# Dynamic filter's taps multiplied for two chunks at once, with the first two pairs' sums copied by the scalar engine and added by GpSimd

## The chip, the cores and the metric

The kernel runs on one core of one Trainium2 chip. The metric is the device time of one execution in microseconds (us). The engines are called PE (matmul), DVE (vector), ACT (scalar), POOL (GpSimd) and SP (sync, which issues the transfers here).

## The reference

The input x is (8, 64, 56, 56). Four layers follow each other, each as x = x + layer(groupnorm(x)):

- layer 0, the dynamic filter: nine taps t of a 3x3 window; the output is the sum over t of patch_t(x) * cf[b, c, t] * sf[b, t, pixel]. cf is a filter per channel from a small network on the pooled x, sf a filter per pixel from a 1x1 convolution. Both are normalised over the nine taps.
- layer 1: a 1x1 convolution times a sigmoid attention map.
- layer 2: a 3x3 convolution with ternary weights.
- layer 3: softmax attention over all 3136 pixels.

```python
def _ddf_mul(x, cf, sf):
    xp = jnp.pad(x, ((0, 0), (0, 0), (1, 1), (1, 1)))
    out = jnp.zeros((B, C, H, W), x.dtype)
    for u in range(3):
        for v in range(3):
            patch = xp[:, :, u:u + H, v:v + W]
            out = out + patch * cf[:, :, u, v][:, :, None, None] * sf[:, u * 3 + v][:, None]
    return out
```

## The kernel before

Two images of 64 channels fill the 128 partitions, so the batch of 8 is four groups, g = 0 to 3 (a loop for the first three, the last written out). Each group runs layers 0 to 3 in turn. An image of 3136 pixels is cut into NJ = 7 chunks of CH = 448 pixels (8 rows of 56); a chunk fills most of one PSUM bank of 512 float32. Engines are kept in step by semaphores written out by hand; each engine works through its own list in order.

The stage that is changed is the tap stage of layer 0. For each chunk j:

- PE spreads the pixel filter of tap t over the channels (`spread_tap`, L1161: one bf16 matmul into bank t % 3). A spread waits for the product three taps earlier, which frees its bank.
- DVE multiplies it by cf and by the shifted patch of the padded input (`tap`, L595: one SCALAR_TENSOR_TENSOR of 448 elements from PSUM and xnp, into the slice `prod[t]`, which lies in the tile Pb).
- PE adds the products of the even taps (0, 2, 4, 6, 8) in PSUM by matmuls with the identity (`add_tap`, L1169: float32, two passes each). Two banks take turns by chunk (`ACCB + odd`).
- POOL adds the odd taps (1, 3, 5, 7) and the layer's input xin in four additions (L1024, L1026, L1029, L1033; `pu`, which lies in the tile VT).
- DVE adds the two sums into xw (`l0_sum`, L605), between taps 3 and 4 of the next chunk.

There is one `prod` slice for each tap. The product of a tap may be written again for the next chunk when its reader has added the one before: PE for even taps, POOL's first addition for taps 1 and 3, the third for tap 5, the fourth for tap 7. After the last chunk DVE takes the group norm statistics of xw (L484, one per chunk; then L489), and the short chain of layer 1's norm follows: PE (L1106, L1110), DVE, POOL (L1013), DVE (L503). ACT has no work in the tap stage except to load its table for layer 1 (L842). `keep_busy` (L1148) issues matmuls whose result nobody reads while that chain runs. Layer 1 then normalises on ACT (L834) and multiplies on PE (L1204, L1205).

Of the kernel before, what the change touches and what calls it, by code (L numbers as in the profile page):

```python
# [166 lines left out]
def build(nc, x, weights, vectors, cst, out):  # L167
    with ExitStack() as ctx:
# [17 lines left out]
        selb = sb("selb", [3 * PITCH, TAPS, P], BF16)  # L186
# [18 lines left out]
        cf = sb("cf", [P, TAPS])  # L205
# [99 lines left out]
        tap_ready = sem("tap_ready")  # L305
# [4 lines left out]
        l0_done = sem("l0_chunk_done")  # L310
        km_ps = sem("km_in_psum")
        km_ready = sem("km_ready")
        u_ps = sem("u_in_psum")
# [128 lines left out]
        def _(dve):  # L442
# [40 lines left out]
            def chunk_stats(src, j):  # L483
                return nc.vector.bn_stats(st6[:, j, :], src[:, j * CH:(j + 1) * CH])  # L484
# [96 lines left out]
            def group(g, more):  # L581
                n[0] = FRONT_LINKS


                def tap(j, t):
                    k = NJ * g + j
                    dve.wait_ge(tap_ready, TAPS * k + t + 1)

                    if t % 2 == 0:
                        dve.wait_ge(tap_added, PE_TAPS * k + t // 2 + 1)  # L590
                    elif t < 7:
                        dve.wait_ge(pool_step, POOL_STEPS * k + (1 if t < 5 else 3))
                    else:
                        dve.wait_ge(pooltaps, k + 1)
                    nc.vector.scalar_tensor_tensor(  # L595
                        out=rows(prod[:, t, :]), in0=rows(PS[:, t % TAP_BANKS, 0:CH]), scalar=cf[:, t:t + 1],
                        in1=pad_rows_at(xnp, j * (ROWS * PW) + (t // 3) * PW + t % 3, ROWS),
                        op0=ALU.mult, op1=ALU.mult).then_inc(prod_ready, 1)

                def l0_sum(j, odd):  # L600

                    dve.wait_ge(tap_added, PE_TAPS * (NJ * g + j + 2))
                    dve.wait_ge(pooltaps, NJ * g + j + 2)
                    dve.wait_ge(stored, 16 * (NJ * g + 1))
                    nc.vector.tensor_tensor(xw[:, ds(j * CH, CH)], PS[:, ACCB + odd, 0:CH], pu[:, 2, :],  # L605
                                            ALU.add).then_inc(l0_done, 1)

                for t in range(TAPS):
                    tap(0, t)
                with dve.Fori(0, NJ // 2) as i:  # L610
                    for odd in (1, 0):
                        j = 2 * i + 2 - odd
                        for t in range(TAPS):
                            if t == 4:
                                l0_sum(j - 1, 1 - odd)
                            tap(j, t)
                dve.wait_ge(l0_done, NJ * (g + 1) + 1)
                for i in range(NJ - 2):
                    chunk_stats(xw, i)
                l0_sum(NJ - 1, 0)  # L620
                chunk_stats(xw, NJ - 2)


                dve.wait_ge(l0_done, NJ * g + NJ + 2)
                stats(g, 1, chunk_stats(xw, NJ - 1))
# [202 lines left out]
        def _(act):  # L828
# [170 lines left out]
        def _(pool):  # L999
# [95 lines left out]
        def _(pe):  # L1095
            mm = nc.tensor.matmul
            pe.sem_inc(tap_added, PE_TAPS)
            pe.sem_inc(l0_done, 2)
            pe.wait_ge(w_loaded, 3 * 16)
            pe.wait_ge(consts, 2)  # L1100
            pe.wait_ge(setup, 1)
# [42 lines left out]
            def group(g, more):  # L1144
# [9 lines left out]
                    pair_var(g, layer, small)  # L1154
                    keep_busy(meanwhile)

                def spread_tap(j, t):

                    k = NJ * g + j
                    pe.wait_ge(prod_ready, TAPS * k + t + 1)  # L1160
                    mm(PS[:, t % TAP_BANKS, 0:CH], selb[:, t, :], SF[:, ds(j * CH, CH)],  # L1161
                       start=True, stop=True).then_inc(tap_ready, 1)

                def add_tap(j, odd, t):
                    k = NJ * g + j
                    pe.wait_ge(prod_ready, TAPS * k + t + 1 + TAP_BANKS)
                    if t == 0:
                        pe.wait_ge(l0_done, k + 1)
                    mm(PS[:, ACCB + odd, 0:CH], identf, prod[:, t, :], start=(t == 0),  # L1169
                       stop=(t == TAPS - 1)).then_inc(tap_added, 1)  # L1170

                def taps(j, odd, first):
                    for t in range(TAPS):
                        spread_tap(j, t)
                        if t in (1, 2) and not first:
                            add_tap(j - 1, 1 - odd, 4 + 2 * t)
                        if t in (3, 5, 7):
                            add_tap(j, odd, t - 3)

                pe.wait_ge(SF_ready, NJ * (g + 1))  # L1180
                taps(0, 0, True)
                with pe.Fori(0, NJ // 2) as i:
                    taps(2 * i + 1, 1, False)
                    taps(2 * i + 2, 0, False)
# [270 lines left out]
```

## Time and profile before

| | us |
|---|---|
| median of three runs (1804.43 to 1806.83) | 1804.92 |
| the profiled execution, its own time | 1803.89 |
| its span, first to last instruction | 1802.0 |
| busy in the span: PE, DVE, ACT, POOL | 1643.3, 1240.5, 1212.8, 1101.6 |
| tap stage with the norm behind it, from the first tap to the end of L503, groups 0 to 3 | 50.16, 52.14, 51.74, 49.06 |

The span is cut into engine busy times; a busy PE is not PE at its peak, since matmuls are pipelined and overlap. Most of the span is layer 3's attention. The four tap stages take 203 us together, 11% of it. PE has two clock levels, 2.4 and 1.2 GHz: the column PEclk of a stretch is its granted share, 1.00 or 0.50 for a stretch at one level.

### The profile page before, as it was taken

The page shows a single profiled execution, that of the slowest core. Times are in us where ns is not written, and L with a number is a line of the kernel's source. Part 1 is how long each engine was busy: PE and PEld are TensorE (multiplying, and loading weights), DVE is VectorE, ACT ScalarE, POOL GpSimd, SP SyncE. Part 2 cuts the span into 40 slices and gives each one's busy share as a digit, 9 for nine tenths or more (in the row PEclk, how much of TensorE's full clock was granted, in tenths as well). Part 3 has the DMA queues.
Part 4 walks back from the last instruction along what each step waited for, and adds up shares of the span by engine and source line. Part 5 has one row for each costly group of instructions (what it writes and reads, how often), then busy time and mean ns, then how long its engine had stood idle before and what let it go on. Part 6 is the DMA issues. An engine that isn't in the chain of part 4 may idle for free.

```text
span 1802.0 us, 35669 instructions
## 1 busy us (share of the span) xinstructions
PE 1643.3 (91%) x10892; PEld 835.9 (46%) x10892; DVE 1240.5 (69%) x2443; ACT 1212.8 (67%) x2300; POOL 1101.6 (61%) x926
## 2 busy tenths in 40 slices
PE   5987899999889799999988879999998788999997
PEld 4364444444436345444444634444443364444442
DVE  5946777775584777777367478777738648877760
ACT  2045889998403689999731278999972237899995
POOL 2720488789551058888955106888887402688888
PEclk9989999999989899999988899999999899999999
DMA  2004000000000400000000040000000002000000
GB/s 87 0 1 90 2 7 7 7 7 11 8 0 1 90 2 7 7 7 7 12 8 0 1 90 2 7 7 11 8 7 6 0 20 35 2 12 6 7 7 11
DMA packets 12423, 27.16 MB, mean 15 GB/s; under 512 B 4560, under 2 KB 8912, under 8 KB 11728
## 3 DMA queue, kind: packets, MB, share of 16 engines
q1 hardware_dynamic: 12240, 24.92, 5.9%
q8 instruction: 90, 1.47, 0.4%
q14 instruction: 93, 0.76, 0.1%
HBM read 8.73 MB, written 6.42 MB: 8 GB/s over the span
## 4 chain that ended last, share of the span: by engine, by line
PE 59%; issue 15%; POOL 10%; DVE 9%; ACT 6%; POOLq 1%; DVEq 0%; ACTq 0%
PE PS L1315 26%; PE PS L1271 12%; PE PS L1241 12%; DVE nmt L688 4%; ACT Pb L956 2%; POOL VT L1024 2%; POOL VT L1029 2%; POOL VT L1026 2%; PE PS L1213 2%; DVE nmt L681 2%; POOL VT L1033 2%; ACT PS L911 1%; PE PS L1204 1%; POOL accP L1076 1%; PE PS L1205 1%
## 5 line engine op out<-in xcount | busy, mean ns | idle before, releaser
L681 DVE TENSOR_REDUCE nmt<-PS 128x1 f32<-128x448 f32 x1176 | 681.6, 618 | 211.0 <-PE PS L1241 208.0
L1076 POOL TENSOR_TENSOR accP<-accP,Pb 128x512 f32<-128x512 f32 (+1 forms) x532 | 676.7, 1272 | 125.9 <-ACT Pb L956 97.5
L956 ACT ACTIVATE Pb<-PS 128x896 f32<-128x896 f32 (+1 forms) x700 | 637.5, 915 | 128.5 <-PE PS L1271 118.9
L1315 PE MATMUL PS<-Pb,VT 128*64 128x448 f32 x2800 | 659.9, 544 | 4.8 <-ACT Pb L956 4.1
L1241 PE MATMUL PS<-Ka,Qa 96*64 96x448 bf16 x2888 | 499.8, 358 | 23.6 <-ACT PS L911 10.7
L1271 PE MATMUL PS<-Qa,Ka 99*64 99x448 bf16 x2744 | 491.7, 353 | 3.3 <-ACT Pb L956 2.8
L911 ACT ACTIVATE PS<-PS,nmt 128x448 f32<-128x448 f32 x588 | 356.6, 606 | 30.6 <-DVE nmt L688 28.6
L1241 PEld LDWEIGHTS PS<-Ka,Qa 96*64 96x64 bf16 x2888 | 168.3, 110 | 270.9 <-issue 117.6
L1271 PEld LDWEIGHTS PS<-Qa,Ka 99*64 99x64 bf16 x2744 | 168.4, 110 | 241.8 <-issue 187.4
L1315 PEld LDWEIGHTS PS<-Pb,VT 128*64 128x64 f32 x2800 | 194.9, 137 | 102.6 <-ACT Pb L956 30.3
L834 ACT ACTIVATE xnp<-xw,nb,rstd 128x448 f32<-128x448 f32 x56 | 40.5, 750 | 204.5 <-DVE nb L503 204.5
L1069 POOL TENSOR_TENSOR accQ<-Pb 128x512 f32<-128x512 f32 x28 | 35.6, 1270 | 226.4 <-ACT Pb L956 226.4
L595 DVE SCALAR_TENSOR_TENSOR Pb<-PS,cf,xnp 128x448 f32<-128x448 f32 x252 | 154.8, 676 | 17.1 <-PE PS L1161 11.8
L1169 PE MATMUL PS<-Pb,cs 128*128 128x448 f32 x280 | 134.0, 560 | 0.7 <-DVE Pb L595 0.7
L1076 POOL TENSOR_TENSOR accQ<-accQ,Pb 128x512 f32<-128x512 f32 x84 | 106.6, 1269 | 23.0 <-ACT Pb L956 19.0
L911 ACT ACTIVATION_READ_ACCUMULATOR PS<-PS,nmt 128x1 f32 x588 | 117.0, 199 | 0.0
L1013 POOL TENSOR_TENSOR rstd<-ve,mhalf 128x1 f32<-128x1 f32 x16 | 8.8, 548 | 169.5 <-DVE ve L499 169.3
L688 DVE TENSOR_REDUCE nmt<-PS 128x1 f32<-128x448 f32 x196 | 104.7, 607 | 1.5 <-PE PS L1241 1.5
L1161 PE MATMUL PS<-xnf,selb 96*128 (+1 forms) x252 | 83.7, 369 | 15.4 <-issue 6.6
L834 ACT ACTIVATE xnf<-xw,nb,rstd 128x448 f32<-128x448 f32 x28 | 20.7, 752 | 102.5 <-DVE nb L503 102.5
L730 DVE STREAM_TRANSPOSE Rr<-PS 128x448 f32<-128x448 f32 x28 | 18.2, 650 | 72.3 <-PE PS L1285 72.3
L1161 PEld LDWEIGHTS PS<-xnf,selb 96*128 96x128 bf16 x252 | 24.6, 98 | 92.2 <-DVE Pb L595 52.9
(145 smaller groups left out, 1478.4 us busy)
## 6 DMA issues: line engine op xcount, KB each, us to landing
xin<-in_x SPq DMA_DIRECT2D x4, 1568.0 KB, 11.9
out<-xw SPq DMA_DIRECT2D x28, 224.0 KB, 1.9
Qa<-parts SPq DMA_DIRECT2D x24, 168.0 KB, 7.6
Ka<-parts SPq DMA_DIRECT2D x24, 112.0 KB, 3.8
Ka<-parts SPq DMA_DIRECT2D x24, 84.0 KB, 2.6
Qa<-mpt SPq DMA_DIRECT2D x96, 1.3 KB
wz<-in_weights SPq DMA_DIRECT2D x1, 829.0 KB, 8.2
Qa<-parts SPq DMA_DIRECT2D x24, 28.0 KB, 1.9
```

Source lines behind the costliest of these rows:

```text
L595: nc.vector.scalar_tensor_tensor(out=rows(prod[:, t, :]), in0=rows(PS[:, t % TAP_BANKS, 0:CH]), scalar=cf[:, t:t + 1], in1=pad_rows_at(xnp ...
L681: nc.vector.reduce_max(nmt[:, target % 2, b, t:t + 1], PS[0:BLK, bank, 0:CH], X, negate=True).then_inc(mx_free, 1)
L688: nc.vector.reduce_max(nmt[:, 0, b, t:t + 1], PS[0:BLK, i % NJ, 0:CH], X, negate=True).then_inc(first_used, 1)
L834: nc.scalar.activation(dst, rows(src[:, j * CH:(j + 1) * CH]), ACT.Identity, bias=nb[:, :], scale=rstd[:, :]).then_inc(done, 1)
L911: return nc.scalar.activation(PS[0:BLK, bank, 0:CH], PS[0:BLK, bank, 0:CH], ACT.Exp, bias=nmt[:, target % 2, b, t:t + 1], accum_out=sm[:, ...
L956: nc.scalar.activation(Pb[0:r, j % PSLOTS, :, :], PS[0:r, 2 * (k % 2):2 * (k % 2) + 2, 0:CH], ACT.Exp).then_inc(exp_done, 1)
L1076: nc.gpsimd.tensor_tensor((accQ if j < TO_ACCP else accP)[0:r, :, REST:CH], (accQ if j <= TO_ACCP else accP)[0:r, :, REST:CH], Pb[0:r, j % ...
L1161: mm(PS[:, t % TAP_BANKS, 0:CH], selb[:, t, :], SF[:, ds(j * CH, CH)], start=True, stop=True).then_inc(tap_ready, 1)
L1169: mm(PS[:, ACCB + odd, 0:CH], identf, prod[:, t, :], start=(t == 0), stop=(t == TAPS - 1)).then_inc(tap_added, 1)
L1241: last = mm(PS[C * h:C * h + C, bank, 0:CH], Qa[0:KROWS, h, s * CH + b * C:s * CH + b * C + C], Ka[0:KROWS, h, t * CH:(t + 1) * CH], start ...
L1271: ins = mm(PS[c:c + C, 2 * (k % 2) + h, 0:CH], Ka[0:KROWS + 3, h, j * QC + c:j * QC + c + C], Qa[0:KROWS + 3, h, s * CH:(s + 1) * CH], sta ...
L1315: last = mm(PS[C * h:C * h + C, OB, 0:CH], VT[:, j, C * h:C * h + C], Pb[:, j % PSLOTS, h, :], start=(j == 0), stop=(j == NQ - 1))
```

## The change

- The seven chunks become four units: `UNITS = ((0, 1), (2, 3), (4, 5), (6,))`. A tap of DVE is one instruction over both chunks of a unit (896 elements over two PSUM banks), the last unit's over one.
- The spread of a unit is two matmuls into a pair of banks; three pairs (banks 0 to 5) take turns as the three banks did.
- The even taps of a unit are added in one pair of banks, 6 and 7, for all units. Before, two single banks took turns.
- That pair must be emptied before the next unit's first even tap is added. For units 0 and 1 (`COPIED = 2`) ACT copies it to SBUF (`acc`, 896 elements) and POOL adds it to its own sum and writes xw; for units 2 and 3 DVE's `l0_sum` does both as before.
- POOL's four additions are of 896 elements for units 0 to 2. Those of the first two units' sums stand behind its second addition of the next unit.
- The products are nine slices of 896 elements: five in Pb, and accP, accD and two pieces of Qa, which are free in this stage.
- DVE takes the statistics of units 0 and 1 between taps 6 and 7 of units 2 and 3, those of units 2 and 3 after the last tap.
- PE adds even taps in another order: 0 and 2 of a unit behind spreads 4 and 6, 4 behind spread 8, and 6 and 8 behind the next unit's spreads 0 and 1.
- The inner loops over chunks are gone from DVE, POOL and PE; the units are written out.

```diff
-TAP_BANKS = 3
+TAP_SLOTS = 3
+UNITS = ((0, 1), (2, 3), (4, 5), (6,))
+COPIED = 2
...
-        prod = flat[:, 0:TAPS * CH].rearrange("p (t n) -> p t n", t=TAPS)
+        prod = [Pb[:, t, :, :] for t in range(PSLOTS)]
...
-        pu = flat[:, 0:3 * CH].rearrange("p (a n) -> p a n", a=3)
+        pu = flat[:, 0:6 * CH].rearrange("p (a h n) -> p a h n", a=3, h=2)
...
-        att, gated = accP, accD
+        att, gated, acc = accP, accD, accQ
+        prod += [accP, accD] + [Qa[:, h, 0:4 * CH].bitcast(F32).rearrange("p (h n) -> p h n", h=2) for h in range(2)]
...
-        ACCB = 4
+        ACCB = 6
...
+                for u in range(len(UNITS)):
+                    for t in range(TAPS):
+                        if t == 5 and u > COPIED:
+                            l0_sum(u - 1)
+                        if t == 7 and u >= 2:
+                            l0_stats(u - 2)
+                        tap(u, t)
+                l0_stats(len(UNITS) - 2)
+                l0_sum(len(UNITS) - 1)
+                stats(g, 1, l0_stats(len(UNITS) - 1))
...
             def group(g, more):
+                for u in range(COPIED):
+                    act.wait_ge(tap_added, PE_TAPS * (len(UNITS) * g + u + 2))
+                    if u:
+                        act.wait_ge(l0_done, len(UNITS) * g + u)
+                    nc.scalar.activation(acc[:, :, :], PS[:, ACCB:ACCB + 2, 0:CH], ACT.Copy).then_inc(acc_copied, 1)
                 load_table(ACT.Sigmoid)
...
+                    nc.gpsimd.tensor_tensor(part[0], prod[1][:, 0:m, :], prod[3][:, 0:m, :], ALU.add).then_inc(pool_step, 1)
...
+                    nc.gpsimd.tensor_tensor(part[1], part[0], x, ALU.add).then_inc(pool_step, 1)
+                    if 1 <= u <= COPIED:
+                        l0_sum(u - 1)
...
+                    nc.gpsimd.tensor_tensor(part[0], part[1], prod[5][:, 0:m, :], ALU.add).then_inc(pool_step, 1)
...
+                    if u:
+                        pool.wait_ge(l0_done, len(UNITS) * g + u)
+                    nc.gpsimd.tensor_tensor(part[2], part[0], prod[7][:, 0:m, :], ALU.add).then_inc(pooltaps, 1)
...
+                def add_tap(u, t):
+                    k = len(UNITS) * g + u
+                    pe.wait_ge(prod_ready, TAPS * k + t + 1 + TAP_SLOTS)
+                    if t == 0 and u == 0:
+                        pe.wait_ge(ocopy, NJ * g + 1)
+                        pe.wait_ge(recip, NJ * g + 1)
+                    elif t == 0 and u <= COPIED:
+                        pe.wait_ge(acc_copied, COPIED * g + u)
+                    elif t == 0:
+                        pe.wait_ge(l0_done, len(UNITS) * g + u)
+                    for i in range(len(UNITS[u])):
+                        last = mm(PS[:, ACCB + i, 0:CH], identf, prod[t][:, i, :], start=(t == 0), stop=(t == TAPS - 1))
+                    last.then_inc(tap_added, 1)
...
+                        spread_tap(u, t)
+                        if u and t in (0, 1):
+                            add_tap(u - 1, 6 + 2 * t)
+                        if t in (4, 6):
+                            add_tap(u, t - 4)
+                        elif t == TAPS - 1:
+                            add_tap(u, 4)
```

## Rows read from the trace of the kernel before

**Rows 1.** The page: engine, busy us, share of the span, instructions.

```profile
PE 1643.3 (91%) x10892; PEld 835.9 (46%) x10892; DVE 1240.5 (69%) x2443; ACT 1212.8 (67%) x2300; POOL 1101.6 (61%) x926
```

**Rows 2.** Busy time by stretch: the tap stages of groups 0 and 3.

```profile
core 0: us, PE busy (x) PEld busy (x) DVE busy (x) ACT busy (x) POOL busy (x), PEclk, DMA share, GB/s
42.62:92.78 50.16, 44.90 (x139) 19.43 (x137) 46.76 (x84) 0.66 (x2) 32.29 (x29) 0.98 0.00 0
...
1368.10:1417.16 49.06, 43.08 (x137) 18.56 (x137) 46.60 (x85) 0.14 (x1) 34.52 (x31) 0.98 0.01 5
```

**Rows 3.** The same view: one chunk in the middle of the stage.

```profile
60.00:66.04 6.04, 5.90 (x20) 2.60 (x19) 6.03 (x11) 0.00 (x0) 4.54 (x5) 1.00 0.00 0
```

**Rows 4.** The chain that ended last, same stretch: start, us, what.

```profile
63.27 0.81 issue
64.12 1.14 POOL VT L1024
```

**Rows 5.** Timeline of DVE: start, us, what, number; its first tap and one chunk.

```profile
42.62 2.65 DVE L595 SCALAR_TENSOR_TENSOR Pb<-PS,cf,xnp 128x448 f32<-128x448 f32 x4 [3.31 <-PE PS L1161]
...
52.41 5.59 DVE L595 SCALAR_TENSOR_TENSOR Pb<-PS,cf,xnp 128x448 f32<-128x448 f32 x9
57.92 0.61 DVE L605 TENSOR_TENSOR xw<-PS,VT 128x448 f32 x1
```

**Rows 6.** Timeline of PE at half and at full clock.

```profile
43.70 1.70 PE L1169 MATMUL PS<-Pb,cs 128*128 128x448 f32 x2
...
57.01 0.92 PE L1169 MATMUL PS<-Pb,cs 128*128 128x448 f32 x2
57.76 0.54 PE L1161 MATMUL PS<-xnf,selb 96*128 x2
```

**Rows 7.** Groups by line and shape, DVE, whole span: count, busy us, mean ns.

```profile
L595 DVE SCALAR_TENSOR_TENSOR Pb<-PS,cf,xnp 128x448 f32<-128x448 f32 x252 | 154.8, 676 | 17.1 <-PE PS L1161 11.8 <-issue 3.6
...
L653 DVE TENSOR_TENSOR xl<-xnp,xh 128x448 fp32r<-128x448 f32 x28 | 17.6, 628 | 22.2 <-ACT xnp L834 22.1
...
L473 DVE TENSOR_TENSOR wt<-wz,Pb 128x1152 fp32r<-128x1152 f32 x1 | 1.4, 1360 | 0.0
```

**Rows 8.** The same view for POOL.

```profile
L1076 POOL TENSOR_TENSOR accP<-accP,Pb 128x512 f32<-128x512 f32 x504 | 641.4, 1273 | 120.0 <-ACT Pb L956 92.8
...
L1033 POOL TENSOR_TENSOR VT<-VT,Pb 128x448 f32<-128x448 f32 x28 | 31.8, 1135 | 6.6 <-POOL VT L1029 6.6
...
L1056 POOL TENSOR_TENSOR sme<-sm,ef 128x21 f32<-128x21 f32 x28 | 6.5, 232 | 0.0
```

**Rows 9.** Timeline of POOL in the tap stage.

```profile
45.35 1.13 POOL L1024 TENSOR_TENSOR VT<-Pb 128x448 f32<-128x448 f32 x1 [6.69 <-DVE Pb L595]
...
53.36 1.13 POOL L1026 TENSOR_TENSOR VT<-VT,xin 128x448 f32<-128x448 f32 x1 [0.19 <-POOL VT L1024]
54.65 1.13 POOL L1029 TENSOR_TENSOR VT<-VT,Pb 128x448 f32<-128x448 f32 x1 [0.16 <-POOL VT L1026]
56.01 1.14 POOL L1033 TENSOR_TENSOR VT<-VT,Pb 128x448 f32<-128x448 f32 x1 [0.23 <-POOL VT L1029]
```

**Rows 10.** The page's groups: ACT on 896 elements of two PSUM banks.

```profile
L956 ACT ACTIVATE Pb<-PS 128x896 f32<-128x896 f32 (+1 forms) x700 | 637.5, 915 | 128.5 <-PE PS L1271 118.9
```

**Rows 11.** Timeline of DVE behind the last tap.

```profile
85.55 2.72 DVE L484 BATCH_NORM_STATS2 st<-xw 128x6 f32<-128x448 f32 x5
88.19 0.61 DVE L605 TENSOR_TENSOR xw<-PS,VT 128x448 f32<-128x448 f32 x1
88.71 1.14 DVE L484 BATCH_NORM_STATS2 st<-xw 128x6 f32<-128x448 f32 x2
```

**Rows 12.** Timeline of PE: three of its idle gaps (in brackets) in group 0.

```profile
90.29 0.38 PE L1106 MATMUL PS<-mv,cs 128*128 128x1 f32 x2 [3.58 <-DVE mv L489]
...
111.04 0.38 PE L1106 MATMUL PS<-mv,cs 128*128 128x1 f32 x2 [3.69 <-DVE mv L489]
...
145.55 0.50 PE L1106 MATMUL PS<-mv,cs 128*128 128x1 f32 x2 [2.22 <-DVE mv L489]
```

**Rows 13.** Busy time by stretch: behind those three gaps.

```profile
91.10:97.80 6.70, 6.26 (x17) 3.24 (x18) 1.15 (x8) 2.71 (x4) 0.55 (x1) 0.50 0.00 1
...
111.60:118.30 6.70, 6.03 (x18) 3.98 (x18) 2.43 (x7) 4.74 (x8) 0.55 (x1) 0.50 0.00 0
...
145.70:152.40 6.70, 6.39 (x15) 2.18 (x16) 1.31 (x5) 2.60 (x4) 0.55 (x1) 0.50 0.00 0
```

More of the change, by code:

```diff
@@ L309, in build @@
         pooltaps = sem("pool_taps_summed")
-        l0_done = sem("l0_chunk_done")
+        acc_copied = sem("tap_sums_copied")
+        l0_done = sem("l0_unit_done")
         km_ps = sem("km_in_psum")
@@ L582, in group, with tap @@
                 n[0] = FRONT_LINKS
-                def tap(j, t):
-                    k = NJ * g + j
+                def tap(u, t):
+                    k, m = len(UNITS) * g + u, len(UNITS[u])
                     dve.wait_ge(tap_ready, TAPS * k + t + 1)
@@ L594, in tap @@
                         dve.wait_ge(pooltaps, k + 1)
+                    b = 2 * ((TAPS * u + t) % TAP_SLOTS)
+                    x = pad_rows(xnp, UNITS[u][0] * ROWS + t // 3, m * ROWS, t % 3)
                     nc.vector.scalar_tensor_tensor(
-                        out=rows(prod[:, t, :]), in0=rows(PS[:, t % TAP_BANKS, 0:CH]), scalar=cf[:, t:t + 1],
-                        in1=pad_rows_at(xnp, j * (ROWS * PW) + (t // 3) * PW + t % 3, ROWS),
+                        out=prod[t][:, 0:m, :].rearrange("p h (r w) -> p h r w", w=W),
+                        in0=PS[:, b:b + m, 0:CH].rearrange("p h (r w) -> p h r w", w=W), scalar=cf[:, t:t + 1],
+                        in1=x.rearrange("p (h r) w -> p h r w", h=m),
@@ L598, in tap, with l0_sum @@
                         op0=ALU.mult, op1=ALU.mult).then_inc(prod_ready, 1)
-                def l0_sum(j, odd):
-                    dve.wait_ge(tap_added, PE_TAPS * (NJ * g + j + 2))
-                    dve.wait_ge(pooltaps, NJ * g + j + 2)
+                def l0_sum(u):
+                    j, m = UNITS[u][0], len(UNITS[u])
+                    dve.wait_ge(tap_added, PE_TAPS * (len(UNITS) * g + u + 2))
+                    dve.wait_ge(pooltaps, len(UNITS) * g + u + 2)
                     dve.wait_ge(stored, 16 * (NJ * g + 1))
-                    nc.vector.tensor_tensor(xw[:, ds(j * CH, CH)], PS[:, ACCB + odd, 0:CH], pu[:, 2, :],
-                                            ALU.add).then_inc(l0_done, 1)
@@ L608, in group @@
[L608 to L625, printed above, removed]
+                    nc.vector.tensor_tensor(xw[:, j * CH:(j + m) * CH].rearrange("p (h n) -> p h n", h=m),
+                                            PS[:, ACCB:ACCB + m, 0:CH], pu[:, 2, 0:m, :], ALU.add).then_inc(l0_done, 1)
+                def l0_stats(u):
+                    dve.wait_ge(l0_done, len(UNITS) * g + u + 1)
+                    for j in UNITS[u]:
+                        last = chunk_stats(xw, j)
+                    return last
@@ L1019, in group, with l0_sum @@
             def group(g, more):
-                with pool.Fori(0, NJ) as j:
-                    k = NJ * g + j
+                def l0_sum(u):
+                    j = UNITS[u][0]
+                    pool.wait_ge(acc_copied, COPIED * g + u + 1)
+                    pool.wait_ge(pooltaps, len(UNITS) * g + u + 2)
+                    pool.wait_ge(stored, 16 * (NJ * g + 1))
+                    nc.gpsimd.tensor_tensor(xw[:, j * CH:(j + 2) * CH].rearrange("p (h n) -> p h n", h=2),
+                                            acc[:, :, :], pu[:, 2, :, :], ALU.add).then_inc(l0_done, 1)
@@ L1022, in group @@
+                for u in range(len(UNITS)):
+                    k, j, m = len(UNITS) * g + u, UNITS[u][0], len(UNITS[u])
+                    x = xin[:, j * CH:(j + m) * CH].rearrange("p (h n) -> p h n", h=m)
+                    part = [pu[:, a, 0:m, :] for a in range(3)]
                     pool.wait_ge(pooltaps, k + 1)
-                    pool.wait_ge(prod_ready, TAPS * k + 4 + TAP_BANKS)
-                    nc.gpsimd.tensor_tensor(pu[:, 0, :], prod[:, 1, :], prod[:, 3, :], ALU.add).then_inc(pool_step, 1)
+                    pool.wait_ge(prod_ready, TAPS * k + 4 + TAP_SLOTS)
+                    nc.gpsimd.tensor_tensor(part[0], prod[1][:, 0:m, :], prod[3][:, 0:m, :], ALU.add).then_inc(pool_step, 1)
@@ L1029, in group @@
-                    nc.gpsimd.tensor_tensor(pu[:, 0, :], pu[:, 1, :], prod[:, 5, :], ALU.add).then_inc(pool_step, 1)
+                    pool.wait_ge(prod_ready, TAPS * k + 6 + TAP_SLOTS)
+                    nc.gpsimd.tensor_tensor(part[0], part[1], prod[5][:, 0:m, :], ALU.add).then_inc(pool_step, 1)
                     pool.wait_ge(pool_step, POOL_STEPS * (k + 1) + 3)
-                    pool.wait_ge(prod_ready, TAPS * k + 8 + TAP_BANKS)
-                    pool.wait_ge(l0_done, k + 2)
-                    nc.gpsimd.tensor_tensor(pu[:, 2, :], pu[:, 0, :], prod[:, 7, :], ALU.add).then_inc(pooltaps, 1)
+                    pool.wait_ge(prod_ready, TAPS * k + 8 + TAP_SLOTS)
@@ L1155, in pair_stats, with spread_tap @@
                     keep_busy(meanwhile)
-                def spread_tap(j, t):
-                    k = NJ * g + j
+                def spread_tap(u, t):
+                    k = len(UNITS) * g + u
                     pe.wait_ge(prod_ready, TAPS * k + t + 1)
[L1161 to L1170, printed above, removed]
@@ L1172, in taps @@
-                def taps(j, odd, first):
-                    for t in range(TAPS):
[L1174 to L1184, printed above, removed]
@@ L1185, in group @@
-                add_tap(NJ - 1, 0, TAPS - 3)
-                add_tap(NJ - 1, 0, TAPS - 1)
+                    for i, j in enumerate(UNITS[u]):
+                        last = mm(PS[:, 2 * ((TAPS * u + t) % TAP_SLOTS) + i, 0:CH], selb[:, t, :],
+                                  SF[:, j * CH:(j + 1) * CH], start=True, stop=True)
+                    last.then_inc(tap_ready, 1)
+                def add_tap(u, t):
+                    k = len(UNITS) * g + u
+                    pe.wait_ge(prod_ready, TAPS * k + t + 1 + TAP_SLOTS)
[9 more added lines that the diff above has]
+                    last.then_inc(tap_added, 1)
@@ new lines, in group @@
+                pe.wait_ge(SF_ready, NJ * (g + 1))
+                for u in range(len(UNITS)):
+                    for t in range(TAPS):
+                        spread_tap(u, t)
[5 more added lines that the diff above has]
+                            add_tap(u, 4)
+                add_tap(len(UNITS) - 1, 6)
@@ L1189, in group @@
+                add_tap(len(UNITS) - 1, 8)
                 pair_stats(1, 2)
```

5 lines of the change are left out of this document (1 added, 4 removed).

## The prediction

> **What bounds the kernel now.** I began with the page [rows 1]: PE is busy 91% of the span, but the change touches only the tap stages, so their limit has to be read there. The busy times by stretch give four stages of 49 to 52 us [rows 2] (the first and last of the four); DVE is busy 46.6 to 46.8 us of each, PE 43 to 45, POOL 32 to 35. In one chunk of 6.04 us in the middle [rows 3] DVE is busy 6.03, PE 5.90, POOL 4.54. The chain of waits runs through POOL's additions there [rows 4], but POOL has spare time (1.5 us a chunk) and DVE none, so I take DVE as the limit, PE as almost level with it, and POOL as third. The timeline of DVE [rows 5] gives the interval at which it starts taps: the nine taps take 5.59 us, which holds one stall of 0.18 for PE; (5.59 - 0.18 - 0.68) / 8 = 0.59 us. The sum L605 holds it another 0.53. Everything below is a price list for three engines that stand close together: what counts is which one comes out last.
>
> **DVE.** Its trace has no tap of 896 elements. A TENSOR_TENSOR takes 628 ns for 448 elements and 1360 for 1152 [rows 7]: 1.04 ns for one more element. So a tap of a pair ends 0.676 + 0.467 = 1.14 us after its start and the next can start 0.59 + 0.47 = 1.06 after. Bounds: 1.06 (that slope) to 1.18 (two taps of before, no gain). I take 1.06, since it is one stream of the same kind. Saved: 0.12 us for each of 27 taps, 3.4 us a stage. Of the seven sums (0.53 each, 3.7) DVE keeps one of a pair and one single (0.99 + 0.53): 2.2 saved. The statistics are moved, not removed.
>
> The Trainium skill ("VectorE: DVE Perf Modes", section on the TRN2 errata) charges a fixed term for each vector instruction beside one cycle an element, and advises tiles of 512 elements or more. By its PSUM figure a pair's tap is 1.06 us as well; this trace agrees for 448 (0.59). Read alone, it speaks for the change, by the whole 5.6 us a stage.
>
> **PE.** Two passes of an addition start 0.38 apart and spreads 0.19 apart at full clock [rows 6] (the ends of two less 0.54 and 0.35). A pair of chunks needs 18 spreads and 20 passes before and after: 18 x 0.19 + 20 x 0.38 = 11.0 us, against the 12.1 that two chunks take now. So 1.1 us a pair is all that can be won while PE is in step, not DVE's 2.5.
>
> **POOL.** Additions take 1.135 us for 448 elements and 1.273 for 512, and 0.232 for 21 [rows 8]: 2.16 ns an element by the near pair, 2.11 by the far one. 896 elements cost 2.08 to 2.10 us; at most 2.27 (two of before). With the gap of 0.16 to 0.23 to the next dependent addition [rows 9], 2.28 each. Units 1 and 2 now have five such additions each, since the sums of units 0 and 1 came to POOL: 11.4 us. That is more than PE's 11.0 and more than DVE's 9.5 to 10.6. POOL becomes the pace of units 1 and 2.
>
> The same skill's "GPSIMD Engine Reference", section Elementwise, gives a GpSimd add of 2048 elements as 4497 ns against 2293 on the vector engine and says to keep elementwise work on the latter. An estimate from that page is 2.06 us for 896: the trace agrees within 2%, and ten additions would end 0.4 us earlier, which changes nothing below.
>
> **ACT.** A copy of 896 elements costs about 0.92 us [rows 10] (another function over the same kind of bank pair). It starts when a unit's tap 8 is added, behind spread 1 of the next, and ends near spread 4, before PE needs the banks: hidden by the spreads and DVE's multiplications. The table load behind both copies has over 20 us of idle ACT to hide in.
>
> **One stage, step by step** (0 = first tap, group 0's clock).
> 1. Unit 0: tap 3 ends at 3 x 1.06 + 1.14 = 4.3; POOL's four additions run from 4.4 to 13.3. DVE's nine taps end at 10.0, with 0.4 lost to PE.
> 2. Unit 1: tap 0 starts at 10.1. Taps 1 and 2 start only at 12.0 and 13.9: in PE's order the four passes of products 6 and 8 (1.5 us each) stand before spreads 1 and 2. Tap 3 ends at 16.05.
> 3. POOL starts its unit 1 at 16.1 and is not idle again before unit 3: ten additions (four of unit 1, four of unit 2, the sums 0 and 1) at 2.28, the last without its gap, end at 38.7. Products 5 and 7 are there in time.
> 4. DVE has multiplied taps 0 to 4 of unit 3 by 37.4 and then waits for POOL in `l0_sum(2)`: 38.9 to 40.0. Queued behind it on DVE are taps 5 to 8; waiting for it on PE is the first addition of unit 3, since the accumulator pair is the only one. PE's last spread ended at 35.7, so PE is idle for 4.3 us.
> 5. Then PE adds product 0 (0.76), spreads tap 5 (0.35), DVE multiplies taps 5 and 6, takes two statistics (1.1), multiplies 7 and 8, PE adds 8, DVE sums (0.61) and takes the last statistic: 7.2 us, end at 47.2.
>
> Before, from the first tap (42.62) to the end of the last statistic (88.71 + 1.14) it is 47.2 us [rows 5, 11]. What the pairs win (11.4 for 12.1) and the shorter tail wins (2.4 us behind the last tap instead of 4.2) goes in the late start of POOL's unit 1 and the stop in unit 3. The first tap itself starts 0.2 to 0.4 us later, as two spreads stand ahead of it (at half clock in group 0, [rows 6]). The same steps with the clocks of the other groups give 0.4, 0.8 and 0.7. Sum: +0.4 +0.4 +0.8 +0.7 = **+2.2 us**, if PE keeps its clock.
>
> **The clock.** After idle gaps of 3.58, 3.69 and 2.22 us [rows 12] the granted clock was 0.50, the 1.2 GHz level, for 6.7 us or more [rows 13]; the half-clock stretches begin 2.4 to 4.4 us behind the start of their gaps. The gap of step 4 (4.3 us) is longer than all three, so I expect the fall at about 38 to 40, and the half clock to last until 45 to 47. All of step 5 then runs on a slow PE: an addition takes 1.5 instead of 0.76 [rows 6]. Of the 7.2 us PE's own work is 10 passes and 4 spreads, 4.6 us, 9.1 at half clock. Followed through, the end moves to 48.7 (fall at 38.0) to 49.5 (at 40): +1.5 to 2.3, I take +1.9 a stage, **+7.6 us** in all. The layer 1 stage starts in half clock now [rows 13]; behind the new tail the gap is 1.9 us instead of 3.6, so it may escape that, worth 4 passes x 0.38 = 1.5 us a stage; or the second fall comes later and covers more of it. I take nothing.
>
> The Trainium skill's "TensorE: Matmul & The Clock Gate", section on HAM oscillation, says that a PE waiting in every tile re-throttles and starts each next one cold; the gap rows agree here (0.50 after all three). By it the price is paid in all four groups, which is my sum; without it the sum stays at +2.2.
>
> **Sum.** +2.2 + 7.6 = +9.8 against the profiled execution's own 1803.9 (span 1802.0): 1813.7. The median of the runs lies 1.0 above that execution, so 1814.7. With the small chance of relief in layer 1 I say 1814.
>
> **The rivals.** A change under 0.2%, 3.6 us, can't be told from none.
> - *Forecast*: POOL paces units 1 and 2, PE waits in unit 3, its clock falls. +5 to +15 us: 1810 to 1820. Chance 0.58.
> - *The gap but no fall, or the fall paid back in layer 1*: for it, the gap sits between stretches of full work, while those of [rows 12] are followed by small matmuls; against it, its length. +2.2, down to -1: about 1806. Chance 0.22.
> - *PE sets the pace, faster*: it decides if an addition of 896 elements costs POOL 1.85 us or less, against 2.08 from both slopes. Then `l0_sum(2)` ends with DVE's own queue, at 38.4 instead of 40.0, which is -1.6 against step 4; the four stages come to -4.2, and 1800.7, if the clock holds too (PE's gap is still 2.7 us). Chance 0.08.
> - *The change does what the instruction counts say*: DVE stays the limit, 5.6 x 4 = -22 us, 1782. It needs PE under 9.6 us a pair, against 11.0. Chance 0.04.
> - *Worse*: the written-out code or the shared accumulator adds stops that I don't see, or half clock reaches through layer 1 as well (+1.5 to 3 a stage more): 1820 to 1826. Chance 0.08.
>
> Faster by over 0.2%: 0.12; within: 0.22; slower: 0.66. The range runs from 1804 (below the second case, without the faster ones) to 1820; the likeliest case alone has 1810 to 1820.
>
> **What would show it.** After the change: taps of 1.14 us, POOL additions near 2.10 us, ten in a row with gaps of 0.2 and not idle from tap 3 of unit 1 on; a DVE wait for POOL before L605's first instance; an idle PE of about 4 us in front of the first addition of unit 3, ended by DVE; PEclk 0.50 in the stretch behind it; a stage about 2 us longer in each group. Wrong would be: a POOL idle in unit 2 (then PE or DVE leads), a gap under 2 us, or a clock of 1.00 behind it.

## The result, and the profile after

The changed kernel took 1809.49 us (median of 10 runs, 1808.10 to 1811.42) beside 1805.94 us of the kernel before (10 runs). The ratio is 1.0022, 95% interval 1.0012 to 1.0031: slower by 0.2%, 3.5 to 4 us. A repeat on another chip gave 1809.4 beside 1804.28, ratio 1.0026 (1.0015 to 1.0036). The forecast was 1814, 9 us slower. The direction was right; the size was not: 3.5 us, and 5.1 in the repeat, for 9. The time lies inside the stated range, just under its likeliest part, 1810 to 1820.

The page has the sums. DVE's busy time fell by 22 us against [rows 1], and nothing was won by it:

```profile
PE 1650.7 (91%) x10892; PEld 844.9 (47%) x10892; DVE 1218.1 (67%) x2315; ACT 1222.9 (68%) x2311; POOL 1108.6 (61%) x886
```

The four tap stages by stretch, from the first tap to the end of the norm chain, the lines that answer to [rows 2]. They end 0.07 us later in the chain than those (at L633, behind L507):

```profile
core 0: us, PE busy (x) PEld busy (x) DVE busy (x) ACT busy (x) POOL busy (x), PEclk, DMA share, GB/s
42.99:94.58 51.59, 45.18 (x138) 20.96 (x136) 41.52 (x52) 3.44 (x6) 34.07 (x19) 0.93 0.00 1
486.43:539.21 52.78, 45.41 (x138) 20.53 (x136) 41.53 (x52) 3.35 (x5) 34.09 (x19) 0.89 0.02 5
933.27:986.03 52.76, 45.58 (x138) 21.04 (x136) 41.53 (x52) 3.35 (x5) 34.07 (x19) 0.88 0.02 5
1374.51:1423.57 49.06, 41.41 (x134) 19.32 (x134) 41.11 (x53) 3.35 (x5) 36.37 (x21) 0.96 0.01 5
```

DVE is busy 5.1 to 5.5 us less in each (41.5 for 46.7), close to the 5.6 by instruction counts, and yet three stages are 0.6 to 1.4 us longer and the fourth is level. A tap of a pair takes 1.14 us, and the next starts 1.05 to 1.06 behind it, both as forecast:

```profile
60.55 1.14 DVE L601 SCALAR_TENSOR_TENSOR accP<-PS,cf,xnp 128x896 f32<-128x896 f32 x1
61.60 1.14 DVE L601 SCALAR_TENSOR_TENSOR accD<-PS,cf,xnp 128x896 f32<-128x896 f32 x1
```

POOL's timeline, group 0, units 1 and 2 and the start of unit 3, answers to [rows 9]:

```profile
59.65 2.09 POOL L1047 TENSOR_TENSOR VT<-Pb 128x896 f32<-128x896 f32 x1 [3.43 <-DVE Pb L601]
61.81 2.08 POOL L1049 TENSOR_TENSOR VT<-VT,xin 128x896 f32<-128x896 f32 x1
63.86 2.08 POOL L1038 TENSOR_TENSOR xw<-accQ,VT 128x896 f32<-128x896 f32 x1
65.91 2.08 POOL L1054 TENSOR_TENSOR VT<-VT,accP 128x896 f32<-128x896 f32 x1
68.20 2.09 POOL L1059 TENSOR_TENSOR VT<-VT,Qa 128x896 f32<-128x896 f32 x1 [0.22 <-POOL VT L1054]
70.73 2.09 POOL L1047 TENSOR_TENSOR VT<-Pb 128x896 f32<-128x896 f32 x1 [0.43 <-DVE Pb L601]
...
79.28 2.07 POOL L1059 TENSOR_TENSOR VT<-VT,Qa 128x896 f32<-128x896 f32 x1 [0.22 <-POOL VT L1054]
81.52 1.13 POOL L1047 TENSOR_TENSOR VT<-Pb 128x448 f32<-128x448 f32 x1 [0.17 <-POOL VT L1059]
```

An addition of 896 elements takes 2.08 us, as forecast. The five of unit 1 start 59.65 and those of unit 2 start 70.73: 11.08 us. POOL waited 0.43 us for a tap at that place, so POOL is not the pace alone; the run e4_noxin below shows that PE is level with it. The last addition of unit 2 ends 38.4 us behind the first tap (forecast 38.7). What waits for it is seen on DVE and then on PE:

```profile
79.14 1.87 DVE L601 SCALAR_TENSOR_TENSOR Pb<-PS,cf,xnp 128x448 f32<-128x448 f32 x3 [0.96 <-PE PS L1187]
81.58 1.09 DVE L613 TENSOR_TENSOR xw<-PS,VT 128x896 f32<-128x896 f32 x1 [0.58 <-POOL VT L1059]
85.15 0.68 DVE L601 SCALAR_TENSOR_TENSOR accP<-PS,cf,xnp 128x448 f32<-128x448 f32 x1 [2.48 <-PE PS L1187]
```

```profile
78.65 0.73 PE L1187 MATMUL PS<-xnf,selb 96*128 96x448 bf16 x3
82.82 1.83 PE L1202 MATMUL PS<-Pb,cs 128*128 128x448 f32 x2 [3.43 <-DVE xw L613]
84.44 0.95 PE L1187 MATMUL PS<-xnf,selb 96*128 96x448 bf16 x2
```

PE stands idle for 3.43 us, released by DVE's sum. Its two passes then take 1.83 us, the 1.70 of half clock [rows 6] rather than the 0.92 of full; DVE in turn waits 2.48 us for tap 5's spread. The stretches behind the gap in groups 0 and 1, each followed by the next:

```profile
81.90:88.60 6.70, 5.78 (x10) 2.79 (x11) 4.22 (x8) 0.00 (x0) 3.46 (x4) 0.50 0.00 1
88.70:95.40 6.70, 3.78 (x17) 1.58 (x15) 3.67 (x13) 0.85 (x2) 1.13 (x2) 1.00 0.00 1
95.60:102.20 6.60, 6.60 (x13) 3.12 (x13) 1.13 (x3) 2.95 (x5) 0.67 (x1) 0.50 0.00 0
...
529.10:532.30 3.20, 3.20 (x7) 1.21 (x6) 1.79 (x4) 0.00 (x0) 1.55 (x2) 0.50 0.00 0
532.50:539.10 6.60, 3.97 (x15) 1.63 (x13) 4.82 (x14) 0.00 (x0) 1.68 (x2) 1.00 0.00 1
539.30:546.00 6.70, 6.70 (x15) 3.42 (x16) 1.14 (x5) 3.66 (x6) 0.00 (x0) 0.50 0.00 0
```

The clock falls as forecast, but in group 1 it is back after 3.4 us, and so it was in groups 2 and 3. The last row of each three is layer 1, where it falls again, later than in the kernel before: compare 95.60 to 102.20 with 91.10 to 97.80 [rows 13]. The fall comes over 4 us later, though the norm chain ends only 1.7 us later.

### The profile page after: what moved, and what is told of

Its sections match the earlier page's. It is cut to its first block, busy times and chain, and to the rows that moved or that the text cites. A ratio compares the mean times of both kernels' runs of the same rounds, so it can differ in the third digit from the quotient of the medians.

```text
span 1809.6 us, 34535 instructions
## 1 busy us (share of the span) xinstructions
PE 1650.7 (91%) x10892; PEld 844.9 (47%) x10892; DVE 1218.1 (67%) x2315; ACT 1222.9 (68%) x2311; POOL 1108.6 (61%) x886
## 4 chain that ended last, share of the span: by engine, by line
PE 66%; issue 13%; DVE 9%; ACT 6%; POOL 5%; DVEq 0%; ACTq 0%; POOLq 0%
PE PS L1345 26%; PE PS L1301 12%; PE PS L1271 12%; PE PS L1202 4%; DVE nmt L695 4%; PE PS L1187 2%; ACT Pb L968 2%; PE PS L1243 2%; DVE nmt L688 2%; PE PS L1234 2%; POOL accP L1102 1%; ACT PS L923 1%; PE PS L1235 1%; PE PS L1153 1%; PE PS L1256 1%
## 5 line engine op out<-in xcount | busy, mean ns | idle before, releaser
L1345 PEld LDWEIGHTS PS<-Pb,VT 128*64 128x64 f32 x2800 | 195.8, 137 | 102.4 <-ACT Pb L968 30.2
L601 DVE SCALAR_TENSOR_TENSOR Pb<-PS,cf,xnp 128x896 f32<-128x896 f32 (+1 forms) x80 | 78.8, 1028 | 26.0 <-PE PS L1187 25.8
L1202 PE MATMUL PS<-Pb,cs 128*128 128x448 f32 x168 | 82.0, 608 | 13.5 <-DVE xw L613 13.5
L1187 PE MATMUL PS<-xnf,selb 96*128 96x448 bf16 x252 | 70.3, 397 | 11.7 <-issue 6.5
L871 ACT ACTIVATE accQ<-PS 128x896 f32<-128x896 f32 x8 | 7.3, 917 | 103.5 <-PE PS L1202 103.5
```

Source lines behind the costliest of these rows:

```text
L601: nc.vector.scalar_tensor_tensor(out=prod[t][:, 0:m, :].rearrange("p h (r w) -> p h r w", w=W), in0=PS[:, b:b + m, 0:CH].rearrange("p h (r ...
L1187: last = mm(PS[:, 2 * ((TAPS * u + t) % TAP_SLOTS) + i, 0:CH], selb[:, t, :], SF[:, j * CH:(j + 1) * CH], start=True, stop=True)
L1202: last = mm(PS[:, ACCB + i, 0:CH], identf, prod[t][:, i, :], start=(t == 0), stop=(t == TAPS - 1))
L1345: last = mm(PS[C * h:C * h + C, OB, 0:CH], VT[:, j, C * h:C * h + C], Pb[:, j % PSLOTS, h, :], start=(j == 0), stop=(j == NQ - 1))
```

## The experiments

Each run is given beside its own runs of the kernel before on the same chip; those medians were 1804.3 to 1804.8. "The tail" is the time from the start of DVE's sum of unit 2 to the start of the aggregation L493, read from the timelines.

**The clock behind the gap (e1_fill).** In `add_tap`, ahead of its waits:

```diff
+                    if t == 0 and u == len(UNITS) - 1:
+                        for _ in range(16):
+                            mm(PS[:, 1, 0:CH], identb[0:3 * PITCH, :], ...)
                     pe.wait_ge(prod_ready, TAPS * k + t + 1 + TAP_SLOTS)
```

> The changed kernel with 16 matmuls whose result nobody reads, put on PE in front of the first addition of unit 3, where PE was idle for 3.4 us (into bank 1, which nothing uses then). At full clock they take about 3.0 us. Theory (the half clock behind that gap is part of the loss): PEclk 1.00 in unit 3, the stage of group 0 ends 1.5 us sooner, the others 0.5 to 1.5 sooner, the total 2 to 6 us under the changed kernel's 1809.5. Rival (the loss is POOL's late sum alone, the clock costs nothing): no change, 1809.5.

1805.43 beside 1804.54, ratio 1.0005 (0.9996 to 1.0014). That is 3 to 4 us under the changed kernel, whose ratio was 1.0022 and 1.0026. Behind the filled gap:

```profile
80.64 3.19 PE L1195 MATMUL PS<-selb,identb 96*128 96x448 bf16 x16
84.23 0.99 PE L1206 MATMUL PS<-Pb,cs 128*128 128x448 f32 x2 [0.40 <-DVE xw L613]
...
85.44 0.92 PE L1206 MATMUL PS<-Pb,cs 128*128 128x448 f32 x2
```

```profile
80.60:91.40 10.80, 8.26 (x32) 3.58 (x29) 8.68 (x14) 0.00 (x0) 6.62 (x5) 1.00 0.00 1
91.60:101.60 10.00, 9.24 (x22) 4.56 (x23) 2.30 (x11) 3.96 (x6) 0.55 (x1) 0.50 0.00 1
```

The first addition of unit 3 waits for the sum as before, but PE's clock holds, and the tail is 8.50, 8.49, 8.50 and 8.42 us. In the changed kernel it is 10.26, 9.13, 9.05 and 9.25, and in its repeat 9.05, 9.24, 10.52 and 9.05. The half clock of unit 3 thus costs 1.8 to 2.0 us where it lasted 6.8 us (one group in each trace) and 0.55 to 0.83 where it lasted 3.4 (three in each): 3.8 and 3.9 us in all. The theory holds, and its size is half of what I had put in. Filling the gap did not mend what follows: in three groups the half clock now began at the end of the stage, the norm chain took 3.15 us for 2.74, and layer 1 was as slow as in the changed kernel.

**The third sum on ACT and POOL too (e2_copied3).** `COPIED = 3`.

> The changed kernel with COPIED = 3: ACT copies the third pair's sum as well and POOL adds it. PE's first addition of unit 3 then waits for a copy of 0.92 us only. Theory (what costs is that the single pair of banks is emptied late, behind POOL's last addition): PE's gap of 3.4 us and the half clock in unit 3 are gone; POOL carries 2.1 us more at the end, so the stage ends 0.5 us later than with the gap at full clock, about 1 us before what was measured; total 1805 to 1807. Rival (POOL's load sets the end): the stage ends 2.1 us later than now, total near 1817.

1807.32 beside 1804.54, ratio 1.0012 (1.0003 to 1.0022). The gap is gone (PE waits 0.44 us for ACT's copy), and POOL's extra addition is in the way at the end instead:

```profile
82.49 1.14 DVE L488 BATCH_NORM_STATS2 st<-xw 128x6 f32<-128x448 f32 x2
...
86.08 1.15 DVE L488 BATCH_NORM_STATS2 st<-xw 128x6 f32<-128x448 f32 x2 [1.27 <-POOL xw L1038]
88.71 0.62 DVE L613 TENSOR_TENSOR xw<-PS,VT 128x448 f32<-128x448 f32 x1 [1.48 <-POOL VT L1059]
```

Moving work to POOL moves the wait. From the first spread to the aggregation L493 the four stages come to 195.6 us together; in the kernel before it is 195.8, in the changed one 200.1. So the pairs win nothing here, and lose nothing, up to that point. The total is at the upper end of the 1805 to 1807 that the theory named, or just above it.

**Nothing moved (e3_copied0).** `COPIED = 0`: the pairs alone, all sums on DVE.

> The changed kernel with COPIED = 0: pairs alone, all four sums by DVE between taps 4 and 5 of the next unit, nothing moved to ACT or POOL. POOL has four additions a unit instead of five. Theory (single pair of banks): PE waits about 4 us in every unit for the sum, the stage grows by 5.7 us at full clock and more with half clock, total 1832 or more. Rival (POOL's load is what costs): POOL is relieved of 4.2 us a stage and the total falls under 1809.

1850.08 beside 1804.54, ratio 1.0249 (1.0235 to 1.0263). PE's gaps, one in each unit behind the first:

```profile
62.48 3.02 PE L1202 MATMUL PS<-Pb,cs 128*128 128x448 f32 x4 [3.78 <-DVE xw L613]
79.13 2.60 PE L1202 MATMUL PS<-Pb,cs 128*128 128x448 f32 x4 [3.78 <-DVE xw L613]
93.80 1.83 PE L1202 MATMUL PS<-Pb,cs 128*128 128x448 f32 x2 [2.76 <-DVE xw L613]
```

All are followed by half clock (3.02 us for four passes, 1.67 at full). The rival by which POOL's load alone is the cost is out: POOL has 4.2 us a stage less than in the changed kernel, and the kernel is 41 us slower than that one. The copy on ACT is what makes a single pair of banks bearable; where it is missing, for unit 3, the change stops.

**POOL without the layer input (e4_noxin).** POOL's second addition is taken out, so this kernel leaves the layer's input out of its result.

> The changed kernel without POOL's addition of the layer input in all units (the residual of layer 0 is left out of the result): POOL has 2.1 us less in units 0 to 2 each. Theory (POOL's lateness holds back the third pair's sum): POOL idles in units 1 and 2, the sum of unit 2 starts at DVE's own place, 1.0 to 1.3 us earlier, PE's gap falls from 3.4 to some 2.5 us and is still followed by half clock; total 1804 to 1806. Rival (PE sets the pace and POOL only follows): the interval between units 1 and 2 stays 11.1 us and the end of the stage moves by less than 0.3 us; total 1809.

1806.55 beside 1804.54, ratio 1.0014 (1.0005 to 1.0023). POOL idles 2.13 us ahead of unit 2 and the interval of the units stays at 11.07 us (60.87 to 71.94), so in units 1 and 2 PE is the pace, even with POOL free. DVE's sum of unit 2 starts in its turn, without a wait for POOL, the gap shrinks from 3.43 to 2.76 us and the clock still falls for 3.4 us. Both theories are right in a part: PE paces the middle, POOL decides the last 0.6 us before the gap's end. The total is 0.5 us above the 1804 to 1806 of the first theory.

**Another bank for the last unit (e5_bank_late, e6_bank).** The single-chunk unit leaves banks 1, 3 and 5 free. Its even taps go to bank 1, and PE's wait for the sum goes:

```diff
-                    elif t == 0:
-                        pe.wait_ge(l0_done, len(UNITS) * g + u)
...
-                        last = mm(PS[:, ACCB + i, 0:CH], identf, prod[t][:, i, :], start=(t == 0), stop=(t == TAPS - 1))
+                        last = mm(PS[:, acc_bank(u) + i, 0:CH], identf, prod[t][:, i, :], start=(t == 0), stop=(t == TAPS - 1))
```

`acc_bank(u)` is 1 for the last unit, else ACCB, in `l0_sum` too. The first run also moves DVE's sum from tap 5 to tap 7 of unit 3.

> The changed kernel with the last unit's even taps added in bank 1, which no spread of the single-chunk unit uses, so that PE does not wait for the third pair's sum; and with DVE's sum of unit 2 between taps 6 and 7 of unit 3 in place of 4 and 5. Theory (the one accumulator pair and the gap it makes are the loss; POOL and PE as measured otherwise): no PE gap in unit 3, PEclk 1.00, the stage of group 0 ends 3.5 to 4 us earlier than in the changed kernel, the others 2.5 to 3.5; total 1794 to 1799, under both kernels. Rival (POOL's backlog sets the end whatever the banks): the end moves by under 1 us a stage, total 1804 or more.

> The bank alone: as the run before it, but DVE's sum of unit 2 stays between taps 4 and 5. PE has no accumulator wait; DVE still waits some 0.6 us for POOL and holds taps 5 to 8 back by that and its own 1.1 us. Theory: most of the gain is PE's gap and its clock, so the total lies 0 to 3 us above the run with both edits, 1796 to 1801. Rival (what is queued behind the sum on DVE is the loss): within 2 us of the changed kernel's time.

Both edits: 1798.0 beside 1804.83, ratio 0.9959 (0.9946 to 0.9972). The bank alone: 1796.26, ratio 0.9950 (0.9938 to 0.9963). Both beat both kernels. The later sum brought nothing, a miss of mine: the bank alone, expected 0 to 3 us above the run with both, is 1.7 under it. Unit 3 with the bank alone:

```profile
79.69 0.92 PE L1204 MATMUL PS<-Pb,cs 128*128 128x448 f32 x2
80.44 0.85 PE L1191 MATMUL PS<-xnf,selb 96*128 96x448 bf16 x2
81.13 0.92 PE L1204 MATMUL PS<-Pb,cs 128*128 128x448 f32 x2
81.89 0.35 PE L1191 MATMUL PS<-xnf,selb 96*128 96x448 bf16 x1
83.78 0.36 PE L1191 MATMUL PS<-xnf,selb 96*128 96x448 bf16 x1 [1.55 <-DVE accP L605]
```

PE goes on at once behind its last spread at full clock. From the sum of unit 2 (82.05) to the aggregation (89.00) it is 6.95 us, 1.5 under the filled gap. From the first spread to the aggregation the four stages come to 190.0 us together, 5.8 under the kernel before.

**The tail's clock (e7_tail, e8_bank_late_tail, e9_bank_tail, e10_bank_tail_more, e12_before_tail).** Matmuls whose result nobody reads, behind the last addition and in the norm chain:

```diff
+                fill(8)
-                pair_stats(1, 2)
+                pair_stats(1, 6)
...
+                keep_busy(1)
                 pe.wait_ge(km_ready, g + 1)
...
-                keep_busy(2)
+                keep_busy(5)
```

> The changed kernel with 8 matmuls whose result nobody reads between the last addition and the norm's first matmul, and 8 more in the short chain behind it (where there were 6). Unit 3 is as it was. Theory (the fall of the clock behind the shorter tail comes later and covers more of layer 1 than before, which cost 0.2 to 1.2 us a group): PEclk 1.00 over layer 1's matmuls, from the end of the norm chain to ACT's last sigmoid 14 us in place of 16.0 to 16.4; total 3 to 7 us under the changed kernel. Rival (layer 1 is not held by PE's clock): it stays at 16 us and the total at the changed kernel's or above, by the matmuls in the chain.

1802.5 beside 1804.83, ratio 0.9988 (0.9978 to 0.9998): 6 to 7 us under the changed kernel. ACT in layer 1, first the changed kernel, then this run:

```profile
94.55 2.72 ACT L841 ACTIVATE xnp<-xw,nb,rstd 128x448 f32<-128x448 f32 x4 [24.07 <-DVE nb L507]
100.10 0.64 ACT L883 ACTIVATE accP<-PS,uc 128x448 f32<-128x448 f32 x1 [2.84 <-PE PS L1235]
100.64 0.75 ACT L841 ACTIVATE xnp<-xw,nb,rstd 128x448 f32<-128x448 f32 x1
102.79 0.64 ACT L883 ACTIVATE accP<-PS,uc 128x448 f32<-128x448 f32 x1 [1.40 <-PE PS L1235]
```

```profile
94.91 2.72 ACT L841 ACTIVATE xnp<-xw,nb,rstd 128x448 f32<-128x448 f32 x4 [22.85 <-DVE nb L507]
98.83 0.64 ACT L883 ACTIVATE accP<-PS,uc 128x448 f32<-128x448 f32 x1 [1.20 <-PE PS L1242]
99.36 0.75 ACT L841 ACTIVATE xnp<-xw,nb,rstd 128x448 f32<-128x448 f32 x1
100.34 0.63 ACT L883 ACTIVATE accP<-PS,uc 128x448 f32<-128x448 f32 x1 [0.23 <-PE PS L1242]
```

ACT waits 1.20 us for PE's first pair in place of 2.84, and 0.23 in place of 1.40 for the next. From the end of the norm chain to the last sigmoid it is 13.59 us in all four groups; in the changed kernel 16.40, 16.06, 16.22 and 15.91, in the kernel before 15.17, 15.82, 15.61 and 15.17.

> Bank 1, the late sum and the matmuls of the run before together. Theory: both gains add, 1789 to 1795. Rival: if the fill matmuls cost more in the chain than the clock gives back, it is above the run with the bank and the late sum alone.

1801.22 beside 1804.83, ratio 0.9980 (0.9968 to 0.9992): worse than without the matmuls (1798.0). The expectation failed. In groups 1 and 2 layer 1 ran at full clock; in groups 0 and 3 the clock had fallen before the tail and stayed at 0.50 for 13.6 us, and the stretch took 17.8 and 17.9 us.

> Bank 1 for the last unit's even taps (DVE's sum between taps 4 and 5, as in the run with the bank alone) and the tail's matmuls together. Theory: in the run with both and the late sum, a PE gap of 1.95 us in unit 3 let the clock fall before the tail, and the tail's matmuls could not hold it in two groups; here that gap is 1.5 us, the clock stays at 1.00 through layer 1's matmuls in all groups, and the total falls by 7 to 9 us under the bank alone: 1787 to 1790. Rival (gaps of 1.5 us are enough for the fall): two groups or more at 0.50 in layer 1, total 1794 or above.

> The run before it with 7 more matmuls whose result nobody reads behind spread 7 of unit 3, where PE waits 1.5 us for DVE. Theory: if the gap there matters to the clock, this holds 1.00 in every group and the total is 1786 to 1789; if not, it equals the run before it within 1 us. They stand before work that DVE waits for only if DVE is early, so they should cost nothing.

1793.42 and 1792.48 beside 1804.28, ratios 0.9935 (0.9922 to 0.9949) and 0.9934 (0.9920 to 0.9947). Layer 1 has 13.59 us in all groups of the first, as expected. The 7 more matmuls (behind spread 7 of unit 3, where PE waited 1.5 us) change nothing in the time that can be told: no clock falls in unit 3 any more, but in group 3 it falls behind the norm chain, and layer 1 takes 15.24 us there. The gain over the bank alone, 2.8 and 3.8 us, was a third to a half of the 7 to 9 us expected. I had worked those out from the trace of e6_bank, and that is of the longest of its five executions: 1798.97 us at a granted clock of 0.962, while the other four took 1795.17 to 1796.85 at 0.968 and 0.969. So the others probably had less half clock to win back than the trace showed.

> The kernel before, with 17 matmuls whose result nobody reads in its gap of 3.6 us behind the last addition and 8 more in the chain. Theory (layer 1's opening is held by the half clock in the kernel before too): from the end of the chain to ACT's last sigmoid 13.6 us in place of 15.2 to 15.8, total 1797 to 1799; so of the gain of the tail's matmuls in the changed kernel (6.3 us) about 3 us make good what the change lost in layer 1 and the rest is not the change's. Rival: layer 1 of before was as fast as it gets, no change, 1804.8.

1797.81 beside 1804.28, ratio 0.9965 (0.9951 to 0.9979), layer 1's stretch 13.59 us in all groups. So the kernel before had this loss too, and the same cure (17 matmuls behind its last addition in place of 8, since its gap there is longer) gives it 6.5 us.

**The changed kernel once more (e11_again).**

> The changed kernel once more, beside a run of before on the same chip: a second trace to see what varies. Theory (where the half clock falls depends on the run): the tap stages differ from the first trace by up to 1.5 us in single groups with the same instructions, full-clock parts agree within 0.1 us, PE's gap in unit 3 is 3.2 to 3.4 us in all four groups again, ratio to before 1.001 to 1.003. Rival (a fixed cost per group): the four stages repeat within 0.3 us.

The gap is 3.44, 3.43, 3.42 and 3.22 us again. The stages from first spread to the end of the chain are 52.96, 53.88, 54.65 and 52.18 us against 52.66, 53.94, 53.82 and 50.71 in the first trace: same instructions, same gaps, up to 1.5 us apart. What differs is where the half clock lies at the stage's start and behind the gap: the first four passes of additions in group 0 take 3.19 us here and 2.48 in the first trace, for 1.67 at full clock.

## Why the prediction came out as it did

The mechanism was forecast step by step and is in the trace: the pair's tap (1.14 us), POOL's addition (2.08), the end of POOL's additions (38.4 for 38.7), the start of the sum (38.6 for 38.9), PE's gap (3.4 for 4.3), the half clock behind it. That the ends agree to 0.3 us is in part luck: POOL began its ten additions 0.6 us later than forecast (16.7 for 16.1) and took 0.9 us less for them (21.7 for 22.6), and in the repeat's group 0 the sum starts at 40.1. One of the forecast's own signs of being wrong is there as well, a POOL that idles in front of unit 2, if only for 0.43 us. The size was not right. From the first spread on, the terms of the forecast against the two traces:

| term | forecast | first trace | repeat |
|---|---|---|---|
| stages with full clock behind the gap | +2.2 | +0.6 | +3.0 |
| half clock in unit 3 | +7.6 | +3.8 | +3.9 |
| norm chain, L493 to the end of L633 (before: L489 to L626) | 0 | -1.2 | -1.2 |
| layer 1 up to the last sigmoid | 0 | +2.8 | +1.4 |
| sum | +9.8 | +6.0 | +7.1 |

The first term is each stage up to the sum of unit 2, plus the tail of the filled run, less the stage of before; the second is the tail less that of the filled run. The forecast's four terms of +2.2 (0.4, 0.4, 0.8, 0.7) add to +2.3. The two traces' spans are 7.6 and 5.8 us longer than that of the trace of before, so 1.6 us more and 1.3 less than these sums lie outside of these stretches, and I can't split them. The medians say +3.5 and +5.1: the first trace is an execution 1.9 us above its median, and that of before is 2.1 and 0.4 under the two medians that it is compared with.

- **The step that failed is the price of the clock, +1.9 us a stage.** I took 6.7 us of half clock from [rows 13], all read at the gap of a norm chain, where matmuls of one column follow. Behind this gap the additions and spreads of the taps follow, and in six of eight stages the half clock lasted 3.4 us, for 0.55 to 0.83 us. In the other two it lasted 6.8 us and cost 1.8 to 2.0, my price. The experiments have 20 more gaps of 2.7 to 3.8 us in front of the same kind of work (12 in e3_copied0, four each in e4_noxin and e7_tail), and behind every one it lasted 3.4 us. What decides between the two lengths stays open. It is not that PE was idle: in layer 1 the half clock lasted 6.8 us with PE busy 6.60 of 6.60, and two stages with the same tap work kept it as long.
- **The full-clock term was right within its scatter** (+0.6 and +3.0 for +2.2), which is wide, since half clock at the start of a stage is in it too. Its parts were a little off: POOL's two additions a unit that don't use the one just before follow with no gap (63.86 to 65.91), where I charged 0.2; so POOL was not the pace alone, PE was level with it (e4_noxin).
- **Layer 1 was put at nothing.** I had named both ways it could go. The second fall comes later and covers more of its matmuls: in the first trace it lasts until 6.6 to 7.8 us behind the chain's end, in the kernel before until 5.1 to 6.4. The chain ahead of it runs at full clock and is shorter (2.74 us for 2.95 to 3.15). Together +1.6 and +0.2. The tail's matmuls (e7_tail) show that the clock is what layer 1 lost by; the filled gap (e1_fill) shows that the gap in unit 3 is not what brought this second fall.
- **The rivals.** The gap with no fall (+2.2) is close to the filled run, which came to +0.9. PE as the pace with POOL free was tried as e4_noxin: PE's gap is 2.76 us, the 2.7 that this rival had, but the clock does not hold, +2.0, so cheaper additions alone would not have made the change faster, as that rival had it. The instruction count's 22 us are won on DVE and nowhere else.
- **What I overlooked** is that the gap has a free cure: a bank that the last unit does not use. With it the same pairs are 0.5% faster than before, 1796.26, and with the tail's matmuls 1792.5 to 1793.4, against 1797.8 for the kernel before with such matmuls of its own. So pairing is worth 4 to 5 us when its accumulator is not in the way and the tail's clock is mended in both kernels.

## What to carry to other kernels

When the next engine stands close behind the busiest (here PE with 5.90 us of a chunk and DVE with 6.03), taking work off the busiest wins only down to the next: 5.1 to 5.5 us of DVE time a stage bought 1 us a pair at most. A merged buffer pair is a new wait; follow each of its emptyings to the end of the stage, and look for a bank that the last, smaller unit leaves free. Price a clock fall by gaps that are followed by the same kind of work, and look at what the next stage gets of it. Before a forecast is built on one trace, see from the other executions' times and clocks whether it is a usual one.

## What the runs showed of the hardware that was not expected

- Half clock behind a PE gap of 3.2 to 3.4 us lasted 3.4 us in six stages of the changed kernel and 6.8 in two, with the same instructions. A gap of 1.5 us was followed by no fall in unit 3 of e6_bank, but by one of 3.4 us in groups 1 and 2 of e9_bank_tail; one of 1.95 us was followed by a fall in all four groups of e8_bank_late_tail.
- Matmuls that only fill time can come too late: in e8_bank_late_tail they stood behind a fall, and the clock stayed at 0.50 for 13.6 us with PE busy 13.5 of them:

```profile
83.00:87.00 4.00, 2.05 (x6) 0.77 (x5) 4.00 (x8) 0.00 (x0) 3.54 (x4) 1.00 0.01 2
87.30:100.90 13.60, 13.49 (x38) 6.42 (x37) 3.19 (x14) 2.71 (x4) 0.73 (x2) 0.50 0.00 1
```

- POOL starts an addition 0.04 us before the last one's end when it does not read its result (2.04 us from start to start at 2.08 each), and 0.08 to 0.22 us behind it when it does (0.08 for the addition of the input, 0.22 for the fourth).
